# Feature attention enters with two tiles summed, and the last stage's first products in another order and rotation of banks

## The chip, the cores and the metric

The kernel runs on one core of one Trainium2 chip. A core has a matmul engine (TensorE, PE in the profile; its weight loads are PEld), a vector engine (VectorE, DVE), an activation engine (ScalarE, ACT), a general engine (GpSimd, POOL) and a queue engine that here only starts transfers (SyncE, SP). The metric is the device time of one execution in microseconds. All times in the rows below are microseconds from the start of one profiled execution.

## The reference: what is computed

Eight layers are applied to x, a residual of 1024 tokens by 256 features, each as x = x + layer(layernorm(x)). The three that the change touches are the last ones:

```
# layer 5: mixture of 8 experts, top 2, y = W2(silu(W1 x) * (W3 x)) for each
out = sum over the two experts of weight * y
# layer 6: attention over the feature axis
qk = einsum('bdm,bdn->bmn', qh, kh) * scale
ret = einsum('bmn,bcn->bcm', softmax(qk), vh)
# layer 7: product-key memory beside a gated MLP
routing = hidden @ W_q against 2 x 64 keys, top 8 of each side, top 8 of the 64 sums
ew = silu(x @ down_embed[indices]) * softmax(scores)
out = (silu(x @ gate_w) * (x @ up_w)) @ down_w + ew @ up_embed[indices]
```

## The kernel before, in words

The program is straight-line code for five engines, each with an instruction stream of its own in hand-written order; they are tied by counting semaphores. The tokens are eight tiles (t = 0 to 7) of 128. The residual X stays in SBUF. The semaphore `x_tile` counts tiles of X that a stage has finished, eight for each.

**End of the experts (layer 5).** The last expert rows are scattered to DRAM (`yg`), and SP brings them back in token order, one transfer for each tile (`sp_last`, L894), into a ring of four places; the fifth and later wait until a place was consumed. DVE then adds, for each tile, two weighted rows to X: `combine(t)`, two `scalar_tensor_tensor` of 128x256, L1063 and L1064, the second after a wait for the first. `combine` is handed to the next stage if `k.front.get(6)` is true. Layer 6 sets `k.front[6] = {}` when it is built; an empty dictionary counts as false in Python. So in the kernel before, all eight `combine(t)` run at the end of layer 5, and `x_of(t)` in layer 6 does nothing.

**Feature attention (layer 6).** For each tile there are four units u (32 in all), and for each unit four scores steps on PE (`scores`, L2326) whose row maxima DVE takes (`top`, L2181, 128x512 out of a bank). Five units of scores (20 steps, `FRONT`) are made before the first unit's softmax; the steps from the 17th on share three banks, so that a step waits for the `top` three steps earlier. DVE's order is: `x_of(0)`, the layernorm statistics of tile 0 (L262 to L264), `x_of(1)`, the normalisation of tile 0 (L281, after POOL's L270 made 1/sqrt), statistics of tile 1, the 20 `top`, `x_of(2)`, `x_of(3)`, and then per unit u four more `top` in two halves, with `rest(u, half)` behind each half; its first line is `x_of(u + 4)` behind the second half of units 0 to 3. PE turns scores for exponentials (`turned`, L2351), and multiplies by the values (L2372). POOL makes masked copies of keys (L2111) and queries (L2118) and folds in the maxima (`less`, L2126).

**Last stage (layer 7).** A gate-up unit n (16 of them: eight for the first 512 tokens, eight for the others, `gate_up(n)`) is two products of 128x512, gate and up, each two matmuls of 128 rows deep; every float32 matmul stands in the trace as two records, so a unit is 8 records, half a unit 4. They go to two banks: `SETS[n % 3]` is bank 0, 2 or 6. ACT makes `silu(n)` (L2682), DVE `product(n)` (L2554), which frees the banks and counts up `h`. `embed(n)`, 4 records, is the product with the expert table, followed by `silu_e(n)` on ACT (L2686). `project(n)` makes the queries (banks 6 and 7, then `q_ps`), ACT copies them (L2714), PE multiplies them by the keys in 32 small matmuls (L2823, banks 6 and 7 again), ACT copies the result (L2718, `r_sb`). DVE's order is fixed: product 0, then for each half of the tiles `sides`, a product, `both`, a product, `places`, a product (so products 1, 2, 3 and then 4, 5, 6 lie between the steps of the top-8 search), then `hot(0)`, product 7 and so on. ACT takes part in this: table loads for `exp`, and `hot` (L2703, L2707), two at a time between the silus. `front_turn(e, 7)` is the transposition of the last tile (L2492), `front_rows` the copy behind it (L2502). `mm` (L354) is the helper that issues every gate-up, project and embed matmul.

The weights of the last stage (4.2 MB) are loaded by SP as soon as `x_tile` says that layer 5 is complete.

Of the kernel before, what the change touches and what calls it, by code (L numbers as in the profile page):

```python
# [21 lines left out]
ALU = mybir.AluOpType  # L22
ACT = mybir.ActivationFunctionType
AX = mybir.AxisListType

P = 128
# [324 lines left out]
def mm(e, out, pairs, start=True, stop=True):  # L351

    for n, (a, b) in enumerate(pairs):
        ins = e.matmul(out, a, b, start=start and n == 0, stop=stop and n == len(pairs) - 1)  # L354
    return ins
# [419 lines left out]
def experts(k, l, F, chunk, row, base, shared_expert, prefix):  # L775
# [164 lines left out]
    def dve(e):  # L940
# [123 lines left out]
            e.scalar_tensor_tensor(k.X[:, t], both[:, 1], wB[:, t:t + 1], k.X[:, t], ALU.mult, ALU.add)\  # L1064
                .then_inc(k.x_tile, 1)

        if not shared_expert and k.front.get(6):
            k.front[6]["combine"] = combine
            return
        for t in range(NT):  # L1070
# [946 lines left out]
def feature_attention(k, l):  # L2017
# [146 lines left out]
    def dve(e):  # L2164
        ch = k.chain(e, "dve")
        front = k.front.get(7)

        def norm(t):
            if t >= 2:
                after(e, "s_ps", STEPS * UNITS * (t - 1))  # L2170
                after(e, "xm", t - 1)
            ln_norm_dve(e, k, at0 + t, t, t % 2).then_inc(k.ln_out, 1)

        def top(u, r):
            t, b, jp = halves(u)
            step = STEPS * u + r
            if t >= 2 and u % UNITS == 0 and r == 0:
                after(e, "nt_ps", t - 1)
            after(e, "s_ps", step + 1)
            c = r * R + 2 * G * (1 - jp)  # L2180
            e.tensor_reduce(nm[t % 2][:, b, c:c + 2 * G:G],  # L2181
                            k.bank[:, step_bank(step), :].rearrange("p (j n) -> p j n", j=2), AX.X, ALU.max,
                            negate=True).then_inc(S["mx"], 1)

        def inverse(t, half):
            after(e, "od", t + 1)
            c = slice(half * P, (half + 1) * P)
            ch.step(e.reciprocal(rec[:, c], od[:, D + half * P:D + (half + 1) * P]))

        def quotient(t):  # L2190
            e.tensor_tensor(tmp, od[:, 0:D], rec, ALU.mult).then_inc(S["v_sb"], 1)

        def final(t):
            after(e, "v_sb", t + 1)
            e.tensor_tensor(k.X[:, t, :], k.X[:, t, :], tmp, ALU.add).then_inc(k.x_tile, 1)

        def rest(u, half):

            t, n = divmod(u, UNITS)
            if half == 1 and u < UNITS:  # L2200
                x_of(u + 4)
            if n == 0 and half == 0 and t + 2 < NT:
                ln_stats_dve(e, k, ch, t + 2, t % 2)
            if n == 1 and half == 0 and t + 2 < NT:
                norm(t + 2)
            if n == 2 and t > 0:
                inverse(t - 1, half)
            if n == 3 and t > 0:
                quotient(t - 1) if half == 0 else final(t - 1)
            if front:  # L2210
                for f, tiles in front["dve_behind"].get((u - LAST, half), ()):
                    for t in tiles:
                        front[f](e, t)

        def x_of(t):

            if k.front.get(6):
                k.front[6]["combine"](t)
                e.wait_ge(k.x_tile, done0 - NT + t + 1)

        e.wait_ge(k.masks, masks0 + 2)
        x_of(0)
        ln_stats_dve(e, k, ch, 0, 0)
        x_of(1)
        norm(0)
        ln_stats_dve(e, k, ch, 1, 1)
        for u in range(FRONT):
            for r in range(RG):
                top(u, r)
            if u == 0:  # L2230
                norm(1)
        x_of(2)
        x_of(3)
        for u in range(NU):
            ahead = [(n, r) for n in units_ahead(u) for r in range(RG)]
            for half in (0, 1):
                for n, r in ahead[half * len(ahead) // 2:(half + 1) * len(ahead) // 2]:
                    top(n, r)
                rest(u, half)
        inverse(NT - 1, 0)  # L2240
        inverse(NT - 1, 1)
        quotient(NT - 1)
        final(NT - 1)
        if front:
            front["stats"](e, NT - 1)
            front["norm"](e, NT - 1)
# [189 lines left out]
def peer_mlp(k, l):  # L2436
# [67 lines left out]
    if l >= 6:  # L2504
# [2 lines left out]
                                      (3, 0): (("stats", (4, 5)), ("norm", (0, 1))), (3, 1): (("norm", (2, 3)),),  # L2507
                                      (5, 1): (("norm", (4, 5)), ("stats", (6,)), ("norm", (6,)))})

    def rows(j, h):  # L2510

        return g["out"].rearrange("(j p h) d -> j h p d", p=P, h=2)[bass.ds(j, 1), h].rearrange("j p d -> p (j d)")
# [35 lines left out]
    def dve(e):  # L2548
        ch = k.chain(e, "dve")

        def product(n):
            half, ib = n // IB, n % IB
            e.wait_ge(S["silu"], n + 1)
            e.tensor_tensor(hT[:, half, ib], sg[n % 3], k.bank[:, SETS[n % 3] + 1, :], ALU.mult).then_inc(S["h"], 1)  # L2554

        def sides(b):
            for u in range(UB * b, UB * b + UB):
# [119 lines left out]
    def act(e):  # L2677
        def silu(n):
            e.wait_ge(S["g_ps"], n + 1)
            if n >= 3:  # L2680
                e.wait_ge(S["h"], n - 2)
            e.activation(sg[n % 3], k.bank[:, SETS[n % 3], :], ACT.Silu).then_inc(S["silu"], 1)  # L2682

        def silu_e(n):
            e.wait_ge(S["e_ps"], n + 1)
            e.activation(eT[:, n // EB, n % EB], k.bank[:, SETS[n % 3], :], ACT.Silu).then_inc(S["e_sb"], 1)  # L2686

        def exp(b):
            r = slice(UB * b, UB * b + UB)
# [55 lines left out]
        for n in range(24, MINE * NT, 2):  # L2745
            hot(n, 2)

    def gate_up(e, n):
        half, ib = n // IB, n % IB
        if n == IB:  # L2750
            e.wait_ge(S["e_sb"], EB)
        if n == 2:
            e.wait_ge(S["r_sb"], 2)
        if n >= 3:
            e.wait_ge(S["h"], n - 2)
        for b in (0, 1):
            ins = mm(e, k.bank[:, SETS[n % 3] + b, :],
                     [(wgu[:, kb, 2 * (ib // 4) + b, ib % 4 * P:(ib % 4 + 1) * P],
                       k.XNT[:, kb, HALF * half:HALF * half + HALF]) for kb in range(KB)])
        ins.then_inc(S["g_ps"], 1)  # L2760

    def project(e, n):
        e.wait_ge(k.xt_sb, at0 + 4 * (n + 1) + CREDIT)
# [3 lines left out]
    def pe_first(e):  # L2767

        e.wait_ge(S["ld"], 16 * 6)
        e.wait_ge(k.xt_sb, at0 + 4 + CREDIT)  # L2770
        gate_up(e, 0)
        front_turn(e, 6)
        e.wait_ge(k.f6_out, k.f6_out_at)
        project(e, 0)
        gate_up(e, 1)
        front_turn(e, 7)
        project(e, 1)

    def pe(e):
        bank = k.bank  # L2780

        def embed(n):
            half, eb = n // EB, n % EB
            if n in (0, 1):
                e.wait_ge(S["h"], IB - 1 + n)
            elif n in (4, 5, 6):
                e.wait_ge(S["h"], 2 * IB - 6 + n)
            elif n in (3, 7):
                e.wait_ge(S["e_sb"], n - 2)
            mm(e, bank[:, SETS[n % 3], :], [(de[:, kb, eb * P:(eb + 1) * P], k.XNT[:, kb, HALF * half:HALF * half + HALF])  # L2790
                                          for kb in range(KB)]).then_inc(S["e_ps"], 1)

        def turn_w(u):
# [24 lines left out]
        for h in (0, 1):  # L2818
# [3 lines left out]
                    at, q = j * 2 * K + side * K, side * HALF + j * P  # L2822
                    ins = e.matmul(bank[:, QB + h, at:at + K], qT[r, q:q + P], keys[r, side], start=True, stop=True)  # L2823
            ins.then_inc(S["k_ps"], 1)
        for n in range(2, IB):
            gate_up(e, n)
        for n in range(EB):
            embed(n)
# [161 lines left out]
```

## Time and profile before

| | before |
|---|---|
| median of 3 runs (lowest, highest) | 1143.98 us (1141.27, 1144.33) |
| the profiled execution | 1145.51 us, of which the span of the profile is 1143.8 |
| PE busy in the span | 1036.3 us (91%) |
| DVE busy | 572.9 us (50%) |
| mean granted clock of PE | 0.94 of full speed |
| first `combine` of layer 5 | 832.69 |
| first scores matmul of layer 6 | 843.84 |
| first gate-up unit of the last stage | 1000.36 |
| last DVE instruction | 1141.22 |

The profile is one execution, 1.5 us above the median of the others. Busy shares are averages over eight stages with different limits, so each edit has to be read in its own stage: who waits there, and for whom. The granted clock has two levels, 0.5 (1.2 GHz) and 1.0 (2.4 GHz); a stretch that shows something between saw both.

### The profile page before, as it was taken

The page shows a single profiled execution, that of the slowest core. Times are in us where ns is not written, and L with a number is a line of the kernel's source. Part 1 is how long each engine was busy: PE and PEld are TensorE (multiplying, and loading weights), DVE is VectorE, ACT ScalarE, POOL GpSimd, SP SyncE. Part 2 cuts the span into 40 slices and gives each one's busy share as a digit, 9 for nine tenths or more (in the row PEclk, how much of TensorE's full clock was granted, in tenths as well). Part 3 has the DMA queues.
Part 4 walks back from the last instruction along what each step waited for, and adds up shares of the span by engine and source line. Part 5 has one row for each costly group of instructions (what it writes and reads, how often), then busy time and mean ns, then how long its engine had stood idle before and what let it go on. Part 6 is the DMA issues. An engine that isn't in the chain of part 4 may idle for free.

```text
span 1143.8 us, 17531 instructions
## 1 busy us (share of the span) xinstructions
PE 1036.3 (91%) x6658; PEld 693.6 (61%) x6658; DVE 572.9 (50%) x1312; ACT 367.9 (32%) x687; POOL 258.7 (23%) x330
## 2 busy tenths in 40 slices
PE   5879999989999999979774999999849999998989
PEld 4666699457666767658653677777613443443467
DVE  6986423543434343455385112122166778556791
ACT  3652233232212121204210222122104666736660
POOL 4321431600000000003531222222132453202350
PEclk9995999999999999989985999999956999988999
DMA  9002032210101010065026112101060000020000
GB/s 285 27 2 101 19 97 84 88 38 29 38 14 38 24 38 5 11 229 226 1 99 223 28 33 102 37 28 42 19 227 1 2 1 1 2 73 1 0 10 28
DMA packets 37433, 67.26 MB, mean 59 GB/s; under 512 B 4456, under 2 KB 27080, under 8 KB 35816
## 3 DMA queue, kind: packets, MB, share of 16 engines
q1 hardware_dynamic: 29960, 51.98, 13.4%
q0 software_dynamic: 4080, 11.15, 3.4%
q10 hardware_dynamic: 3312, 3.02, 0.8%
q8 instruction: 56, 0.92, 0.3%
q14 instruction: 25, 0.20, 0.1%
HBM read 54.72 MB, written 11.40 MB: 58 GB/s over the span
## 4 chain that ended last, share of the span: by engine, by line
PE 76%; DVE 14%; ACT 3%; DMA 3%; issue 2%; POOL 2%; SPq 0%; DVEq 0%; ACTq 0%; POOLq 0%
PE bank L354 21%; PE bank L1255 12%; PE bank L1279 7%; PE bank L1605 6%; PE bank L2326 4%; PE bank L2351 3%; PE bank L2372 3%; PE bank L1615 3%; PE bank L2808 2%; PE bank L1268 2%; PE bank L1590 2%; PE bank L1580 2%; PE bank L2390 1%; PE bank L2814 1%; PE bank L1240 1%
## 5 line engine op out<-in xcount | busy, mean ns | idle before, releaser
L1255 PE MATMUL bank<-big 128*128 x552 | 147.7, 417 | 0.6 <-ACT big L1140 0.6
L354 PE MATMUL bank<-XNT,big 128*128 128x512 f32 x296 | 140.7, 626 | 5.4 <-DVE big L2554 2.8
L1255 PEld LDWEIGHTS bank<-big 128*128 128x128 f32 x552 | 98.1, 191 | 39.6 <-issue 2.7
L2326 PE MATMUL bank<-big,xs 32*128 32x512 f32 x256 | 88.5, 739 | 18.7 <-DVE xs L281 17.7
L270 POOL TENSOR_TENSOR rstd<-ve,half 128x1 f32<-128x1 f32 x48 | 27.5, 576 | 331.6 <-DVE ve L264 331.3
L354 PEld LDWEIGHTS bank<-XNT,big 128*128 128x128 f32 x296 | 56.6, 199 | 70.7 <-issue 62.0
L2181 DVE TENSOR_REDUCE big<-bank 128x2 f32<-128x512 f32 x128 | 81.9, 685 | 24.7 <-PE bank L2326 24.1
L1279 PE MATMUL bank<-big 128*128 (+1 forms) x368 | 87.2, 380 | 1.1 <-ACT big L1155 1.1
L1033 DVE TENSOR_TENSOR big<-big,bank 128x704 f32<-128x704 f32 x23 | 20.5, 889 | 124.9 <-ACT big L1148 124.9
L2272 ACT ACTIVATE big<-bank 128x1024 f32<-128x1024 f32 x64 | 64.9, 1024 | 38.9 <-PE bank L2351 38.6
L354 PE MATMUL bank<-CTXT,big 128*128 128x512 f32 (+1 forms) x192 | 67.0, 493 | 10.7 <-DMA big<-wvT 10.7
L1279 PEld LDWEIGHTS bank<-big 128*128 128x128 f32 (+1 forms) x368 | 68.0, 190 | 13.6 <-issue 1.7
L2351 PE MATMUL bank<-big 32*128 32x512 f32 x256 | 69.3, 667 | 1.6 <-POOL big L2126 1.4
L1148 ACT ACTIVATE big<-bank 128x176 f32<-128x176 f32 (+1 forms) x46 | 24.7, 538 | 136.6 <-PE bank L1255 135.8
L1605 PE MATMUL bank<-big 128*128 128x256 f32 x256 | 65.4, 401 | 1.2 <-issue 1.2
L1512 ACT COPY big<-bank 128x1024 f32<-128x1024 f32 x16 | 16.2, 1012 | 145.5 <-PE bank L1615 145.5
L1464 DVE COPY big<-bank 128x512 f32<-128x512 f32 x16 | 11.1, 691 | 99.5 <-PE bank L1590 99.5
L354 PE MATMUL bank<-big,CTXT 128*128 128x256 f32 (+1 forms) x224 | 58.0, 409 | 0.0
L354 PEld LDWEIGHTS bank<-CTXT,big 128*128 128x128 f32 x192 | 32.9, 196 | 40.8 <-issue 40.8
L915 POOL DMA_INDIRECT yg<-big x23 | 22.7, 986 | 150.8 <-DVE big L1046 144.0
L2326 PEld LDWEIGHTS bank<-big,xs 32*128 32x128 f32 x256 | 31.6, 210 | 40.7 <-issue 26.8
L1605 PEld LDWEIGHTS bank<-big 128*128 128x128 f32 x256 | 47.4, 195 | 14.0 <-DVE X L1458 5.4
(351 smaller groups left out, 1807.2 us busy)
## 6 DMA issues: line engine op xcount, KB each, us to landing
big<-m_gu SPq DMA_DIRECT2D x8, 1408.0 KB
big<-m_d SPq DMA_DIRECT2D x8, 768.0 KB
big<-a_qk SPq DMA_DIRECT2D x16, 256.0 KB, 2.9
yg<-big ACTq DMA_DIRECT2D x23, 128.0 KB
big<-m_gu SPq DMA_DIRECT2D x8, 352.0 KB
big<-a_o SPq DMA_DIRECT2D x16, 128.0 KB, 2.1
xn<-XNT SPq DMA_DIRECT2D x8, 256.0 KB, 5.9
big<-f_keys SPq DMA_DIRECT2D x1, 2048.0 KB, 9.1
```

The costliest lines, as they stand in the source:

```text
L270: e.tensor_tensor(k.rstd[at % NT][:, :], k.ve[at % NT][:, :], k.half[:, 0:1], ALU.pow).then_inc(k.ln_rstd, 1)
L354: ins = e.matmul(out, a, b, start=start and n == 0, stop=stop and n == len(pairs) - 1)
L1148: tell(e.activation(dst, src, ACT.Silu), "hs")
L1255: ins = e.matmul(out, xgT[s % 2][:, kb, :], WB[:, bass.ds(at[s] + (kb * 2 * F + c * chunk), chunk)], start=kb == 0, stop=kb == KB - 1)
L1279: ins = e.matmul(bank[:, Y[s % 2], 0:D], hT[s % 2][0:row, b, :], WB[0:row, bass.ds(at[s] + (WGU + b * D), D)], start=b == 0, stop=b == NB - 1)
L1605: ins = e.matmul(bank[:, QK0 + j % 2, q * D:(q + 1) * D], cT[:, t * P:(t + 1) * P], wo[h % 2], start=True, stop=True)
L1615: ins = e.matmul(bank[:, CB + b, t * SEQ:(t + 1) * SEQ], v[rows(b), h % FIRST, t], pT[rows(b), t], start=True, stop=True)
L2181: e.tensor_reduce(nm[t % 2][:, b, c:c + 2 * G:G], k.bank[:, step_bank(step), :].rearrange("p (j n) -> p j n", j=2), AX.X, ALU.max, negate= ...
L2272: e.activation(pt[u % 2][:, r].rearrange("p r j n -> p r (j n)"), k.bank[:, b:b + 2, :], ACT.Exp, scale=float(G) ** -0.5).then_inc(S["ex"], 1)
L2326: e.matmul(bank[:, step_bank(step), :], k.xs[t % 2][q, b * P:(b + 1) * P], cm[t % 2][q, 2 * jp:2 * jp + 2].rearrange("p j n -> p (j n)"), ...
L2351: ins = e.matmul(bank[:, pair_banks(u, pair) + r % 2, :], cr[q, t, jp, nb * P:(nb + 1) * P], xm[t % 2][q, 2 * jp:2 * jp + 2].rearrange("p ...
L2372: ins = e.matmul(bank[r * R:(r + 1) * R, VB, jp * D:(jp + 1) * D], cv[t % 2][:, nb, r * J + 2 * jp + j], pt[u % 2][:, r, j], start=nb == 0 ...
```

## The change

Two parts. First, the test `k.front.get(6)` becomes `6 in k.front` in both places: layer 5 hands over `combine` and returns, and layer 6 makes the sums itself, tiles 0 and 1 at its start, 2 and 3 behind the 20 `top`, and 4 to 7 one behind each of the units 0 to 3. Second, in the last stage, the banks of the gate-up units and of the embed products rotate in another order, half of unit 1 and the transposition of tile 7 change places, and the first half of unit 2 is issued ahead of the product with the keys. The waits follow: unit 2 needs product 0 (it uses banks 0 and 1 now) and no longer the copied routing scores, which unit 3 now waits for; the first embed product needs product 5 and not 6.

```diff
-        if not shared_expert and k.front.get(6):
+        if not shared_expert and 6 in k.front:
             k.front[6]["combine"] = combine
             return
@@
         def x_of(t):
-            if k.front.get(6):
+            if 6 in k.front:
                 k.front[6]["combine"](t)
                 e.wait_ge(k.x_tile, done0 - NT + t + 1)
@@
+    def unit_banks(n):
+        return SETS[n if n < 2 else (0, 2, 1)[(n - 2) % 3]]
+    def embed_bank(n):
+        return SETS[(0, 2, 1)[n % 3 if n < EB else (n + 1) % 3]]
@@ product, silu, silu_e: SETS[n % 3] becomes unit_banks(n), embed_bank(n)
-    def gate_up(e, n):
+    def gate_up(e, n, part=(0, 1)):
-        if n == IB:
-            e.wait_ge(S["e_sb"], EB)
-        if n == 2:
-            e.wait_ge(S["r_sb"], 2)
-        if n >= 3:
-            e.wait_ge(S["h"], n - 2)
-        for b in (0, 1):
+        if 0 in part:
+            if n == IB:
+                e.wait_ge(S["e_sb"], EB)
+            if n == 2:
+                e.wait_ge(S["h"], 1)
+            if n == 3:
+                e.wait_ge(S["r_sb"], 2)
+            if n >= 4:
+                e.wait_ge(S["h"], n - 2)
+        for b in part:
...
-        ins.then_inc(S["g_ps"], 1)
+        if 1 in part:
+            ins.then_inc(S["g_ps"], 1)
@@ pe_first
         project(e, 0)
-        gate_up(e, 1)
+        gate_up(e, 1, (0,))
         front_turn(e, 7)
+        gate_up(e, 1, (1,))
         project(e, 1)
+        gate_up(e, 2, (0,))
@@ embed
-            if n in (0, 1):
-                e.wait_ge(S["h"], IB - 1 + n)
+            if n in (0, 1, 2):
+                e.wait_ge(S["h"], IB - 2 + n)
@@ behind the products with the keys
-        for n in range(2, IB):
+        gate_up(e, 2, (1,))
+        for n in range(3, IB):
             gate_up(e, n)
```

## Rows read from the trace of the kernel before

**Rows 1.** The page, chain of work that ended last, shares of the span.

```profile
PE 76%; DVE 14%; ACT 3%; DMA 3%; issue 2%; POOL 2%; SPq 0%; DVEq 0%; ACTq 0%; POOLq 0%
```

**Rows 2.** Timeline, entry of layer 6: start, us, engine, line, [idle before, releaser].

```profile
832.69 0.48 DVE L1063 SCALAR_TENSOR_TENSOR X<-XNT,big,X 128x256 f32<-128x256 f32 x1 [6.12 <-DMA XNT<-yg]
833.21 0.48 DVE L1064 SCALAR_TENSOR_TENSOR X<-XNT,big,X 128x256 f32<-128x256 f32 x1
...
841.71 0.42 DVE L262 BATCH_NORM_STATS2 st<-X 128x6 f32<-128x256 f32 x1
...
842.49 0.15 DVE L264 TENSOR_SCALAR ve<-mv 128x1 f32<-128x1 f32 x1
...
843.33 0.41 DVE L281 TENSOR_SCALAR xs<-X,mv,rstd 128x256 f32<-128x256 f32 x1 [0.68 <-POOL rstd L270]
...
843.84 5.74 PE L2326 MATMUL bank<-big,xs 32*128 32x512 f32 x22 [17.73 <-DVE xs L281]
```

**Rows 3.** Busy time by stretch in layer 6; behind POOL the granted clock, DMA share, GB/s.

```profile
843.80:856.30 12.50, 10.20 (x32) 4.84 (x32) 10.95 (x20) 0.00 (x0) 9.15 (x20) 0.64 0.84 332
856.30:863.60 7.30, 6.52 (x23) 2.68 (x24) 2.58 (x4) 3.36 (x6) 4.33 (x3) 0.50 0.00 0
863.60:872.50 8.90, 8.90 (x26) 3.82 (x25) 6.67 (x13) 1.94 (x2) 0.56 (x1) 0.50 0.00 0
872.50:890.00 17.50, 17.50 (x147) 5.80 (x146) 11.67 (x21) 11.43 (x15) 6.49 (x8) 0.92 0.00 1
```

**Rows 4.** Timeline of layer 6 where the late sums would stand, DVE and POOL.

```profile
860.94 1.89 POOL L2111 TENSOR_TENSOR big<-big,strip 128x1024 f32<-128x1024 f32 x1
...
863.70 1.89 DVE L2181 TENSOR_REDUCE big<-bank 128x2 f32<-128x512 f32 x3 [1.12 <-PE bank L2326]
...
875.63 1.29 DVE L2181 TENSOR_REDUCE big<-bank 128x2 f32<-128x512 f32 x2 [2.36 <-PE bank L2326]
...
884.70 1.29 DVE L2181 TENSOR_REDUCE big<-bank 128x2 f32<-128x512 f32 x2 [0.49 <-PE bank L2326]
884.77 1.28 POOL L2126 TENSOR_TENSOR big<-big 128x512 f32<-128x512 f32 x1 [1.72 <-ACT big L2262]
```

**Rows 5.** Timeline of the last stage's first 25 us.

```profile
1009.85 1.98 PE L354 MATMUL bank<-XNT,big 128*128 128x512 f32 x4 [0.46 <-ACT XNT L2502]
...
1011.87 0.61 ACT L2714 COPY big<-bank 128x512 f32<-128x512 f32 x1 [1.56 <-PE bank L354]
...
1012.62 3.82 PE L2823 MATMUL bank<-big 64*128 64x64 f32 x32 [0.79 <-ACT big L2714]
...
1017.09 0.23 DVE L2558 MAX8 big<-big 128x8 f32<-128x64 f32 x1 [9.96 <-ACT big L2718]
...
1024.05 0.69 DVE L2554 TENSOR_TENSOR big<-big,bank 128x512 f32<-128x512 f32 x1 [1.41 <-ACT big L2682]
```

**Rows 6.** The chain that ended last, 1000 to 1061 us: start, us, what.

```profile
1000.36 3.43 PE bank L354 x8
...
1017.11 6.21 PE bank L354 x8
...
1035.50 0.69 DVE big L2554
...
1042.61 0.61 DVE big L2554
1043.27 6.79 PE bank L354 x8
...
1050.67 1.22 ACT big L2703 x2
...
1054.16 7.13 PE bank L354 x16
```

**Rows 7.** One line's instructions (ns least/median/most), and POOL's timeline beside it.

```profile
L2594 DVE TENSOR_TENSOR big<-big x2: 191/1061/1931, 1029.2 to 1040.7; 128x32 f32<-128x32 f32 x2
...
1040.22 2.34 POOL L2544 TENSOR_TENSOR big<-big 128x1024 f32<-128x1024 f32 x1 [34.03 <-ACT big L2707]
```

More of the change, by code:

```diff
@@ L2553, in product @@
             e.wait_ge(S["silu"], n + 1)
-            e.tensor_tensor(hT[:, half, ib], sg[n % 3], k.bank[:, SETS[n % 3] + 1, :], ALU.mult).then_inc(S["h"], 1)
+            e.tensor_tensor(hT[:, half, ib], sg[n % 3], k.bank[:, unit_banks(n) + 1, :], ALU.mult).then_inc(S["h"], 1)
         def sides(b):
@@ L2681, in silu @@
                 e.wait_ge(S["h"], n - 2)
-            e.activation(sg[n % 3], k.bank[:, SETS[n % 3], :], ACT.Silu).then_inc(S["silu"], 1)
+            e.activation(sg[n % 3], k.bank[:, unit_banks(n), :], ACT.Silu).then_inc(S["silu"], 1)
         def silu_e(n):
             e.wait_ge(S["e_ps"], n + 1)
-            e.activation(eT[:, n // EB, n % EB], k.bank[:, SETS[n % 3], :], ACT.Silu).then_inc(S["e_sb"], 1)
+            e.activation(eT[:, n // EB, n % EB], k.bank[:, embed_bank(n), :], ACT.Silu).then_inc(S["e_sb"], 1)
         def exp(b):
@@ L2746, in act @@
             hot(n, 2)
-    def gate_up(e, n):
+    def gate_up(e, n, part=(0, 1)):
         half, ib = n // IB, n % IB
-        if n == IB:
-            e.wait_ge(S["e_sb"], EB)
-        if n == 2:
-            e.wait_ge(S["r_sb"], 2)
-        if n >= 3:
-            e.wait_ge(S["h"], n - 2)
-        for b in (0, 1):
-            ins = mm(e, k.bank[:, SETS[n % 3] + b, :],
+        if 0 in part:
[8 more added lines that the diff above has]
+        for b in part:
+            ins = mm(e, k.bank[:, unit_banks(n) + b, :],
                      [(wgu[:, kb, 2 * (ib // 4) + b, ib % 4 * P:(ib % 4 + 1) * P],
                        k.XNT[:, kb, HALF * half:HALF * half + HALF]) for kb in range(KB)])
-        ins.then_inc(S["g_ps"], 1)
+        if 1 in part:
+            ins.then_inc(S["g_ps"], 1)
     def project(e, n):
@@ L2789, in embed @@
                 e.wait_ge(S["e_sb"], n - 2)
-            mm(e, bank[:, SETS[n % 3], :], [(de[:, kb, eb * P:(eb + 1) * P], k.XNT[:, kb, HALF * half:HALF * half + HALF])
+            mm(e, bank[:, embed_bank(n), :], [(de[:, kb, eb * P:(eb + 1) * P], k.XNT[:, kb, HALF * half:HALF * half + HALF])
                                           for kb in range(KB)]).then_inc(S["e_ps"], 1)
```

## The prediction, made before the change was run

> **What bounds the kernel now.** I read the chain that ended last first: three quarters of it is PE [rows 1]. But the change touches only two places where PE is not the bound, so the answer lies in the timeline there. At the entry of layer 6, PE stands still for 17.73 us: DVE waits for the first returned expert row, sums tile 0 from 832.69, and comes to the statistics of tile 0 only at 841.71, behind all eight sums, though they need tile 0 alone; the first scores matmul is at 843.84 [rows 2]. In the last stage the chain changes engine at 1024.05, where DVE waits 1.41 us for the silu of unit 2; from there it is DVE's, through product 5 at 1035.50 to product 6 at 1042.61; PE, out of work, takes up the embed products at 1043.27 and, by way of ACT, unit 8 at 1054.16 [rows 5, 6]. The third view is the granted clock: half speed from 856.3 to past 872.5, because PE was nearly idle before and then waits for banks; only then nearly full [rows 3].
>
> **The dead test.** The dictionary is empty when it is first tested, so before the change nothing is handed over. With the new test the sums of tiles 1 to 7 move. I take them in DVE's order.
>
> Entry. A sum is two dependent instructions, 833.21 - 832.69 = 0.52 us apart, so 1.04 us a tile [rows 2]. Tile 0 is done at 832.69 + 1.04 = 833.73, and the statistics follow at once, 7.98 us earlier than at 841.71. Between the last statistics instruction (842.49 + 0.15 = 842.64) and the normalisation (843.33) DVE idles 0.69 us for POOL's reciprocal root [rows 2]; the sum of tile 1 goes in there with 1.04 us, 0.35 more than the gap. I add 0.5 for POOL's small instruction and the sum getting in each other's way. First scores matmul at 843.84 - 7.98 + 0.85 = 836.7: **7.1 us gained**. It can't be more than 7.98. The weights of the last stage are loaded when the eighth sum is done, now some 35 us later, about 165 us before their first use (1000.36 [rows 6]); that delay costs nothing. With the cover gone it would cost the load's length, about 12 us (DMA share 0.84 in the 12.5 us from 843.8 [rows 3]).
>
> What the six other sums take back (6 x 1.04 = 6.2 us of DVE):
> - Tiles 2 and 3 stand behind the 20th maximum, in front of the one at 863.70. DVE idles 1.12 us before it, so it ended at 862.58; POOL's L2111 runs until 862.83. The two sums end at 862.83 + 2.08 = 864.9, 1.2 late [rows 4]. From here to 872.5 PE's scores at half clock go round three banks, each step waiting for a maximum, and DVE is busy 6.67 of 8.9 us [rows 3]; a delay at the head of such a ring is passed on in full. Cost 1.2.
> - Tile 4 falls ahead of 875.63, where DVE idled 2.36 us [rows 4] and only 0.4 us of normalisation shares the gap. Cost 0.
> - Tiles 5 to 7 fall between pairs of maxima, 872.5 to 890. DVE is busy 11.67 of 17.5 us there [rows 3], idle 0.49 before the pair at 884.70 [rows 4], the sum 1.04. Each overruns by about 0.5, and PE, which is never idle there, can absorb a part. Tile 7 would run beside POOL's L2126 of 884.77 [rows 4], and such neighbours block each other: L2594 takes 0.19 us once and 1.93 the other time, ending as POOL's 1040.22 + 2.34 does [rows 7]. Its second half waits up to 1.3 us. Cost 0.4 + 0.4 + 0.9 = 1.7.
>
> So 2.9 is taken back, **4.2 us net**. Bounds: nothing beyond the 1.2 (net 5.9), and all 6.2 us plus the 1.3 us block (7.5, net -0.4, nothing gained).
>
> The Trainium skill, SBUF — State Buffer, section "SBUF: two separate sides", says the same of the block as a lock: a VectorE instruction with two SBUF inputs and a GpSimd instruction hold a shared port pair for their whole length, and the later one stands still. By that rule every sum that meets POOL pays; with the rule left aside and the sums sliding through beside POOL, the give-back would be 0.25 + 0.9 less and the net 5.3 instead of 4.2. The row on L2594 agrees with the lock.
>
> **The last stage.** At full clock 8 records take 3.43 us, 4 take 1.72 [rows 6].
> - The transposition of tile 7 moves ahead of half a unit, so ACT's copy lies beside PE's work. PE's wait of 0.46 us before project(1) goes: it starts at 1009.4 [rows 5].
> - The first half of unit 2 follows it. Its wait is for product 0, long made. project(1) ends streaming 1.72 us later, 1011.1; the half unit ends at 1012.8; ACT's copy (1011.87 before, 1011.4 now, 0.61 long) is done by then. The 32 small matmuls start at 1012.85 instead of 1012.62 and end at 1016.7 instead of 1016.44 [rows 5]. So the top-8 search starts **0.2 us later** (1017.3).
> - The second half of unit 2 runs at 1016.7 without a wait and ends at 1018.4, at 1020.1 if the clock is down. Before, the whole unit and the next came after 1017.11, took 6.21 us for 8 records that are worth 3.43 [rows 6], and the silu of unit 2 was there just before 1024.05. Now it is there at about 1019.3 (1021 with a slow clock), before DVE wants product 2 at 1022.6 + 0.2. DVE's wait of 1.41 goes, less 0.2: **1.2 us gained** on DVE's chain either way [rows 5].
> - Products 3, 4, 5 then come 1.2 earlier with DVE as the bound, product 5 at 1034.3. Units 6 and 7 wait for products 3 and 4 as before; PE is through unit 7 near 1035.7, and embed(0), which now needs product 5 alone, follows at once and ends near 1037.5. Before, it was the first half of the 6.79 us that began at 1043.27 [rows 6]: at half clock **3.4 us** taken out of the stretch behind product 6.
> - Product 6. DVE's own chain puts it at 1042.61 - 1.2 = 1041.4. POOL's 2.34 us instruction moves too (ACT's `hot` comes some 2 us earlier), and it may block DVE's small steps in another place: 1041 to 1042. I take 1041.4.
> - PE is then idle for about 4 us, so the clock falls, as it had after the shorter wait before. Embed 1 to 3 are 12 records: 7 at half clock (6.0) and 5 at full (2.1) end at 1042.1 + 8.1 = 1050.2, silu 0.7: unit 8 at about 1051. Against 1054.16 this is 3.2. ACT's four `hot` instructions (from 1050.67 [rows 6]) no longer stand between the second and third silu_e at the end, but under embed(2), which itself waits for product 7. I take **3.0 us**. Bounds: 1.2 + 0.5 (only DVE's part and the wait) = 1.7 below, and 5.5 if the clock stays up and the 12 records take 5.2.
>
> Behind unit 8 the banks and waits come out as before, so the rest shifts as a block.
>
> **Sum.** 4.2 + 3.0 = 7.2 us. On the profiled span: 1143.8 - 7.2 = 1136.6 (its own time 1145.51, so 1138.3). The median of the runs is 1.5 below that execution; 1143.98 - 7.2 = **1136.8 us**. Because those runs lie 3.1 us apart, I call 0.3% (3.4 us) the least that can be told from no change.
>
> **Rivals.**
> 1. *The sums take everything back.* DVE is the bound from 843.8 on and the six sums cost their length and the block. For it: 10.95 of 12.5 us busy [rows 3]. Against: none of the six stands in that stretch. Time 1143.98 + 0.4 - 3.0 = 1141.4. Chance 0.08.
> 2. *The last stage gains nothing*, as POOL's instruction moved onto DVE's steps holds product 6 at 1042.6 and the colder PE pays for embed(0). For it: the 1.93 of L2594 [rows 7]. Against: embed(0) is out of the way. 1143.98 - 4.2 = 1139.8. Chance 0.13.
> 3. *More than forecast:* the clock rises earlier in layer 6. From 863.6 to 872.5 PE takes 8.9 us at half clock where DVE has 6.67 us of work [rows 3]; at full clock DVE would set the pace, 2.2 less. With 4.5 in the last stage: 1143.98 - 4.2 - 2.2 - 4.5 = 1133.1. Chance 0.15.
> 4. *Slower:* the clock stays down in layer 6. It rose only shortly after 872.5, where the full mix of matmuls began [rows 3]; if the pauses of PE for the sums of tiles 5 to 7 keep it down, each microsecond of work costs one more, since PE is busy all of the 17.5 us there [rows 3]. 7.2 us of such work undo the gain; from 10.6 us of it on (21 us of further half clock) the kernel is over 3.4 us slower. For the whole stretch, at its clock of 0.92: 1136.8 + 0.84 x 17.5 = 1151.5. Against: PE has no idle there, and the sums add only tenths. Chance 0.03.
>
> The forecast itself has 0.61, with its own range 1134.5 to 1139.5. Rivals 1 and 4 are left outside the range, and half of 3's tail: **1132.0 to 1140.6**. Faster by over 0.3%: below 1140.5, the forecast, rival 3 and most of rival 2: 0.87. Within 0.3%: rival 1 and the rest: 0.10. Slower: 0.03.
>
> **What would show it.** First L1063 near 832.7, then L262 near 833.7, first L2326 near 836.7; eight sums spread to about 878; the 21st maximum 1 us behind its old distance from the entry; the first sort of layer 6 (PE L2390) 4 us earlier. In the last stage, unless shifted: no DVE wait at product 2, four L354 records ahead of L2823, embed(0) ahead of product 6, unit 8 about 3 us closer to unit 0 (53.8 us before). Wrong it would be through a longer half-clock stretch after 863, a stall of PE at the sums of tiles 5 to 7 of over 1 us each, or L2594 blocked again.

## The result, and the profile after

The changed kernel takes 1135.42 us (median of 5 runs, 1134.34 to 1137.76) against 1143.98 of before, timed beside it (5 runs, 1141.27 to 1148.46); the ratio is 0.9931, 95% interval 0.9911 to 0.9951. Measured once more it was 0.9947 (0.9929 to 0.9965). The forecast was 1136.8 us, 7.2 less; by the two ratios the measured gain is 7.9 and 6.1 us. The profiled execution took 1134.34, its span 1132.6. Ratios compare undisturbed executions: one of the six of experiment 8's kernel took 4096 us, for a cause that nothing on record shows, and is left out.

The page of the changed kernel: its first line, and the chain that ended last by engine. It answers to [rows 1]: PE's share of the chain fell, DVE's rose.

```profile
span 1132.6 us, 17536 instructions
...
PE 73%; DVE 17%; issue 3%; DMA 3%; ACT 2%; POOL 2%; SPq 0%; DVEq 0%; ACTq 0%; POOLq 0%
```

**Entry of layer 6**, the timeline of DVE and then of PE, in answer to [rows 2]. In all the rows below, `...` stands for lines left out.

```profile
831.14 0.48 DVE L1063 SCALAR_TENSOR_TENSOR X<-XNT,big,X 128x256 f32<-128x256 f32 x1 [6.44 <-DMA XNT<-yg]
831.66 0.48 DVE L1064 SCALAR_TENSOR_TENSOR X<-XNT,big,X 128x256 f32<-128x256 f32 x1
832.18 0.43 DVE L262 BATCH_NORM_STATS2 st<-X 128x6 f32<-128x256 f32 x1
...
833.56 0.48 DVE L1064 SCALAR_TENSOR_TENSOR X<-XNT,big,X 128x256 f32<-128x256 f32 x1
834.08 0.41 DVE L281 TENSOR_SCALAR xs<-X,mv,rstd 128x256 f32<-128x256 f32 x1
```

```profile
834.59 2.09 PE L2326 MATMUL bank<-big,xs 32*128 32x512 f32 x8 [10.35 <-DVE xs L281]
```

The statistics stand 1.04 us behind the first sum, where they stood 9.02 behind it. The second sum fills DVE's wait for POOL's reciprocal root, and the normalisation follows it without a gap. From the first sum to the first scores matmul it is 3.45 us instead of 11.15 [rows 2].

**The late sums**, DVE's timeline and one line of POOL's, in answer to [rows 4].

```profile
853.25 0.62 DVE L1063 SCALAR_TENSOR_TENSOR X<-XNT,big,X 128x256 f32<-128x256 f32 x1
...
854.94 0.48 DVE L1064 SCALAR_TENSOR_TENSOR X<-XNT,big,X 128x256 f32<-128x256 f32 x1
855.46 1.89 DVE L2181 TENSOR_REDUCE big<-bank 128x2 f32<-128x512 f32 x3
...
867.19 1.29 DVE L2181 TENSOR_REDUCE big<-bank 128x2 f32<-128x512 f32 x2 [1.32 <-PE bank L2326]
...
872.50 0.49 DVE L1064 SCALAR_TENSOR_TENSOR X<-XNT,big,X 128x256 f32<-128x256 f32 x1
873.38 1.29 DVE L2181 TENSOR_REDUCE big<-bank 128x2 f32<-128x512 f32 x2 [0.40 <-PE bank L2326]
...
876.73 0.48 DVE L1064 SCALAR_TENSOR_TENSOR X<-XNT,big,X 128x256 f32<-128x256 f32 x1
876.87 1.48 POOL L2126 TENSOR_TENSOR big<-big 128x512 f32<-128x512 f32 x1 [1.68 <-ACT big L2262]
```

Counted from the first scores matmul, the 21st maximum comes at 20.87 (855.46 - 834.59) where it came at 863.70 - 843.84 = 19.86: 1.0 is given back at the head of the ring. The pair of 867.19 is 0.8 late; the wait ahead of it shrank from 2.36 to 1.32, which is the sum of tile 4. The sum of tile 7 (its second half at 876.73) meets POOL's L2126, but it is the earlier of the two: it takes its usual 0.48 us, and POOL 1.48 where it took 1.28.

**The last stage**, from the chain that ended last, and POOL's timeline beside it, in answer to [rows 6, 7]. The first L354 line is unit 0, the next the embed products 1 to 3, the last unit 8; L2561 is `product` here (the two shown are products 2 and 6), L2595 and L2598 are two of DVE's small steps.

```profile
993.26 3.43 PE bank L354 x8
...
1015.28 0.69 DVE big L2561
...
1030.95 2.07 DVE big L2595
...
1033.05 0.19 DVE big L2596
...
1033.26 1.13 DVE big L2598
...
1034.92 0.61 DVE big L2561
...
1035.57 8.03 PE bank L354 x12
...
1044.27 7.13 PE bank L354 x16
```

```profile
1030.61 2.35 POOL L2551 TENSOR_TENSOR big<-big 128x1024 f32<-128x1024 f32 x1 [31.52 <-ACT big L2714]
1033.04 1.31 POOL L2553 TENSOR_TENSOR big<-big 128x512 f32<-128x512 f32 x1
```

Product 2 stands in the chain of DVE without a wait. Unit 8 comes 1044.27 - 993.26 = 51.0 us behind unit 0, 53.8 before. But two small DVE steps, usually of 0.2 us, end within 0.06 us of POOL's instructions (1033.02 against 1030.61 + 2.35 = 1032.96, 1034.39 against 1033.04 + 1.31 = 1034.35), so product 6 is only 0.6 us nearer to unit 0 (41.66 against 42.25). The embed products, 12 records, take 8.03 us behind a pause of 5.42.

### The profile page after: what moved, and what is told of

The parts are those of the page before. It is cut to its first block, busy times and chain, and to the rows that moved or that the text cites. A ratio compares the mean times of both kernels' runs of the same rounds, so it can differ in the third digit from the quotient of the medians.

```text
span 1132.6 us, 17536 instructions
## 1 busy us (share of the span) xinstructions
PE 1028.8 (91%) x6658; PEld 687.2 (61%) x6658; DVE 574.8 (51%) x1312; ACT 368.4 (33%) x687; POOL 258.8 (23%) x330
## 3 DMA queue, kind: packets, MB, share of 16 engines
q0 software_dynamic: 4080, 11.15, 3.5%
## 4 chain that ended last, share of the span: by engine, by line
PE 73%; DVE 17%; issue 3%; DMA 3%; ACT 2%; POOL 2%; SPq 0%; DVEq 0%; ACTq 0%; POOLq 0%
PE bank L354 20%; PE bank L1255 13%; PE bank L1279 7%; PE bank L1605 6%; PE bank L2326 5%; PE bank L2351 3%; PE bank L2372 3%; PE bank L1615 3%; PE bank L1268 2%; PE bank L1590 2%; PE bank L2821 2%; PE bank L1580 2%; PE bank L2390 1%; DVE big L2608 1%; DMA big<-yg,big 1%
## 5 line engine op out<-in xcount | busy, mean ns | idle before, releaser
L354 PE MATMUL bank<-XNT,big 128*128 128x512 f32 x296 | 136.3, 609 | 6.9 <-DVE big L2561 5.4
L354 PEld LDWEIGHTS bank<-XNT,big 128*128 128x128 f32 x296 | 55.0, 193 | 69.8 <-issue 59.1
L354 PE MATMUL bank<-CTXT,big 128*128 128x512 f32 (+1 forms) x192 | 67.0, 493 | 11.0 <-DMA big<-wvT 11.0
L354 PE MATMUL bank<-big,CTXT 128*128 128x256 f32 (+1 forms) x224 | 57.9, 409 | 0.0
L354 PEld LDWEIGHTS bank<-CTXT,big 128*128 128x128 f32 x192 | 32.9, 196 | 41.2 <-issue 41.1
```

## The experiments

Every kernel was profiled once and timed in five rounds. The table gives, for each profiled execution, four distances read from the timelines: from the first sum to the first scores matmul, from there to unit 0 of the last stage, from unit 0 to unit 8, and from unit 8 to the end of the span. (The timeline puts unit 0 0.16 us earlier than the chain does, so 51.17 here is the 51.0 above, and 53.96 the 53.8.) The ratio is to the kernel before, timed beside it.

| execution | entry | to unit 0 | to unit 8 | to the end | ratio (95%) |
|---|---|---|---|---|---|
| before | 11.15 | 156.36 | 53.96 | 89.64 | |
| before again | 10.20 | 156.79 | 52.60 | 88.29 | 1.0003 (0.9984 to 1.0022) |
| second part alone | 10.34 | 156.72 | 50.41 | 90.92 | 0.9998 (0.9981 to 1.0015) |
| second part alone, again | 10.77 | 156.34 | 50.31 | 89.53 | 0.9993 (0.9975 to 1.0011) |
| rotation alone | 10.32 | 156.70 | 50.17 | 90.92 | 0.9985 (0.9968 to 1.0001) |
| first part alone | 3.45 | 158.70 | 52.65 | 89.65 | 0.9932 (0.9910 to 0.9954) |
| first part alone, again | 3.45 | 158.63 | 50.87 | 88.23 | 0.9946 (0.9930 to 0.9963) |
| changed | 3.45 | 158.51 | 51.17 | 88.33 | 0.9931 (0.9911 to 0.9951) |
| changed again | 3.45 | 158.57 | 51.29 | 88.32 | 0.9947 (0.9929 to 0.9965) |
| sums in gaps | 3.44 | 157.11 | 50.35 | 89.53 | 0.9926 (0.9903 to 0.9949) |
| sums early | 3.45 | 162.92 | 50.65 | 89.44 | 0.9987 (0.9973 to 1.0000) |
| POOL later | 3.45 | 158.57 | 47.59 | 88.28 | 0.9924 (0.9907 to 0.9941) |
| PE kept busy | 3.45 | 158.14 | 49.29 | 89.49 | 0.9944 (0.9927 to 0.9961) |
| all together | 3.45 | 157.09 | 46.47 | 88.33 | 0.9888 (0.9860 to 0.9916) |

**1. The first part alone.** The kernel before with

```diff
-        if not shared_expert and k.front.get(6):
+        if not shared_expert and 6 in k.front:
@@
-            if k.front.get(6):
+            if 6 in k.front:
```

> The kernel before with the first part of the change alone (both tests of the dictionary). Theory (the two parts add up, each by its own mechanism): the changed kernel's trace gives 11.15 - 3.45 = 7.7 us from the first sum to the first scores matmul, and takes 2.15 back before the last stage, so 5.5 us net: 1138.4 us, ratio about 0.995; first L1063 to first scores matmul 3.45 us, unit 0 of the last stage 158.7 us behind the first scores matmul, and 53.8 us from unit 0 to unit 8 as before. Rival (the late sums take everything back and the gain is all the last stage's): 1144, ratio 1.000. Rival (the gain is all the sums'): 1135.5, ratio 0.993.

Entry and way to unit 0 are the changed kernel's to 0.2 us. The gain is 7.8 us where 5.5 were expected, as much as the whole change has: 0.9932. The interval holds 0.995 and 0.993, so neither the theory nor the second rival is out. From unit 0 to unit 8 it is 52.65 and not 53.96: DVE's wait at product 2, 1.41 us in [rows 5], is 0.61 here with the same code. It was run again beside the changed kernel.

> The first part alone once more. Theory: 5.2 us faster than before, ratio 0.9955. Rival (the first part is the whole gain, as the first comparison had it, 0.9932): 0.993.

0.9946, between the two, and the interval holds both. The whole change, run beside it, had 0.9947: in the times the second part adds nothing to the first.

**2. The second part alone.** The changed kernel with both tests set back to `k.front.get(6)`.

> The kernel before with the second part alone (the last stage's order and banks). Theory: from unit 0 to unit 8 51.0 us instead of 53.8, and up to 1.3 behind unit 8, so 2.8 to 4.1 us: 1140.5 us, ratio about 0.997; no wait of DVE at product 2. Rival (no gain, the search on DVE sets product 6 and what the embed products save is lost to the clock): 1144, ratio 1.000.

> The second part alone once more. Theory: 2.5 us faster than before, ratio 0.998; the granted clock falls at the last embed product or not, which decides over up to 3 us of the end (unit 0 to the end 141.3 with the dip, 139.5 without). Rival (nothing, as the first comparison had it, 0.9998): 1.000.

In both traces unit 8 comes at 50.4 and 50.3 behind unit 0, a little earlier than the theory's 51.0, and DVE doesn't wait at product 2. In the times it is not to be seen: 0.9998 and 0.9993, so between 2.2 us faster and 1.7 slower, and between 2.9 faster and 1.3 slower. The first comparison leaves out the theory's 0.997 and had the rival; the second holds both 0.998 and 1.000. Some of the difference is behind unit 8, where the forecast had seen only a block that shifts. PE's timeline of the second part alone, then of the changed kernel, at the last transposition before the down products (L2811), the last embed product (L354) and the first down product (L2821):

```profile
1087.54 0.66 PE L2811 MATMUL bank<-ident,big 128*128 128x128 f32 x4 [2.65 <-DVE big L2616]
1088.03 3.04 PE L354 MATMUL bank<-XNT,big 128*128 128x512 f32 x4
1091.75 5.53 PE L2821 MATMUL bank<-big 128*128 128x256 f32 x16 [0.69 <-ACT big L2693]
```

```profile
1083.55 0.66 PE L2811 MATMUL bank<-ident,big 128*128 128x128 f32 x4 [2.66 <-DVE big L2616]
1084.04 1.88 PE L354 MATMUL bank<-XNT,big 128*128 128x512 f32 x4
1086.61 3.72 PE L2821 MATMUL bank<-big 128*128 128x256 f32 x16 [0.69 <-ACT big L2693]
```

The wait ahead is the same, 2.65 and 2.66 us. In one execution the clock falls and the two pieces (the embed product and the down product) take 3.04 + 5.53 = 8.57 us, in the other it stays and they take 5.60.

**3. The rotation alone.** The second part alone, with the early half of unit 2 and the split of unit 1 taken back:

```diff
-        gate_up(e, 1, (0,))
-        front_turn(e, 7)
-        gate_up(e, 1, (1,))
-        project(e, 1)
-        gate_up(e, 2, (0,))
+        gate_up(e, 1)
+        front_turn(e, 7)
+        project(e, 1)
@@
-        gate_up(e, 2, (1,))
-        for n in range(3, IB):
+        for n in range(2, IB):
```

> The second part with the new rotation of the banks and its waits, but unit 1 whole and unit 2 whole behind the products with the keys, as before. Theory: the early half unit keeps the clock up and makes product 2 ready, the rotation gives embed(0) ahead of product 6; here the clock falls again beside the 32 small matmuls (granted 0.5 in some of the 8 us behind them), DVE waits about 0.8 us at product 2, and embed(0) still comes early: 1.5 to 2.5 us faster than before, so 1141.8, ratio 0.998. Rival (the gain is the early half unit's): 1144, ratio 1.000, embed(0) early or not.

0.9985, 1.7 us faster, within what was expected, though the interval reaches 1.0001; unit 8 is at 50.17, no later than with the early half. The expected wait of DVE at product 2 did not come, though the clock fell as expected (0.67 in the four microseconds from 1012, product 2 is at 1017.6). Unit 2 starts here as soon as the 32 small matmuls are through (1011.32), without the wait of 0.68 us for the copied scores that stands ahead of it in all four executions of the old order: with the new banks unit 3 has that wait. So what the second part gains, if anything, comes with the banks and their waits; moving the half unit adds nothing that shows.

**4. The kernel before, again.**

> The kernel before once more, unchanged: a second profiled execution of it, and what the comparison says of no change. Open is why the second part of the change shows 2.5 us in the traces and next to nothing in the times. Theory (the profiled execution of before had an unlucky clock in the last stage, 143.6 us from unit 0 to the end, where the first part alone had 142.3 and 139.1 without any edit there): this one lies between 139 and 142.5, and the ratio is 1.000 within 0.002. Rival (143.6 is what this stage takes in before, and the second part's gain is real but lost in the times elsewhere): 143.6 within 0.3.

The theory held: the ratio is 1.0003, and the last stage takes 140.9 us here (52.60 + 88.29), 143.6 in the execution on which the forecast was made, 142.3 and 139.1 in the two of the first part alone, which has the same code there. PE's timeline of this execution and then of the first part alone, again, behind the pause that ends with product 6 (embed products, then unit 8):

```profile
1043.05 8.78 PE L354 MATMUL bank<-XNT,big 128*128 128x512 f32 x16 [2.79 <-DVE big L2554]
1052.51 7.13 PE L354 MATMUL bank<-XNT,big 128*128 128x512 f32 x16 [0.69 <-ACT big L2686]
```

```profile
1037.71 1.98 PE L354 MATMUL bank<-XNT,big 128*128 128x512 f32 x4 [2.79 <-DVE big L2554]
1040.66 5.42 PE L354 MATMUL bank<-XNT,big 128*128 128x512 f32 x12 [0.97 <-DVE big L2554]
1046.77 7.13 PE L354 MATMUL bank<-XNT,big 128*128 128x512 f32 x16 [0.69 <-ACT big L2686]
```

The pause is 2.79 us in both and in the first profile of before. Here the four embed products take 8.78 us, there 1.98 + 5.42 with a wait between; in the first profile of before 10.21. So a part of what the second part seemed to win from 53.96 was the clock of that one execution.

A second thing shows when the four executions of the old order are laid beside the new one. In the first part alone, DVE's timeline at product 2, at the long L2594 and at product 6, and then POOL's:

```profile
1016.79 0.69 DVE L2554 TENSOR_TENSOR big<-big,bank 128x512 f32<-128x512 f32 x1 [0.61 <-ACT big L2682]
...
1033.41 1.94 DVE L2594 TENSOR_TENSOR big<-big 128x32 f32<-128x32 f32 x1
1035.27 0.68 DVE L2554 TENSOR_TENSOR big<-big,bank 128x512 f32<-128x512 f32 x1
```

```profile
1032.96 2.35 POOL L2544 TENSOR_TENSOR big<-big 128x1024 f32<-128x1024 f32 x1 [32.77 <-ACT big L2707]
1035.38 1.27 POOL L2546 TENSOR_TENSOR big<-big 128x512 f32<-128x512 f32 x1
```

Product 6 stands 41.07 us behind unit 0 here (1035.27 - 994.20) and 41.08 when run again, 42.34 and 42.41 in the two executions of before. In the changed kernel it is 41.74 and 41.91, in the second part alone 41.88 and 41.90. From product 2 to product 6 it is 18.5 us in all four executions of the old order and 19.6 to 19.7 in these four: the old order has one of POOL's additions ahead of product 6, and the second begins when product 6 has begun (1035.38); the new order has both ahead of it.

**5. Where a late sum costs.** Two kernels, each the changed one with late sums moved. `sums in gaps`: tiles 2 and 3 behind the 16th maximum, 5 behind the normalisation of tile 2; 4, 6 and 7 stay where the change has them, so three of the six move. `sums early`: 2 to 4 behind the 8th maximum, 5 to 7 behind the 12th. The edit of `sums in gaps`, then that of `sums early`:

```diff
-            if half == 1 and u < UNITS:
-                x_of(u + 4)
+            if (u, half) in ((0, 1), (2, 1), (3, 1)):
+                x_of(4 + u)
@@
+            if u == 1 and half == 0:
+                x_of(5)
@@
             if u == 0:
                 norm(1)
-        x_of(2)
-        x_of(3)
+            if u == UNITS - 1:
+                x_of(2)
+                x_of(3)
```

```diff
-            if half == 1 and u < UNITS:
-                x_of(u + 4)
@@
-        x_of(2)
-        x_of(3)
+            if u in (1, 2):
+                for t in (2, 3, 4) if u == 1 else (5, 6, 7):
+                    x_of(t)
```

> The changed kernel with the six late sums moved to where DVE is idle: tiles 2 and 3 behind the 16th maximum (DVE idles 2.78 us there), 4 where it is, 5 behind the normalisation of tile 2 (1.32 idle), 6 and 7 behind units 2 and 3. Theory (the 2.15 us given back are waits of PE for maxima behind the sums, above all the two at the head of the three-bank ring): first scores matmul to unit 0 of the last stage 157.0 instead of 158.7, 1.6 us faster than the changed kernel: 1133.8, ratio to before 0.9915. Rival (the give-back is the clock's, not the sums' place): no change, 1135.4.

> The changed kernel with all six late sums in the stretch where DVE takes maxima back to back (tiles 2 to 4 behind the 8th maximum, 5 to 7 behind the 12th). Theory (there DVE sets the pace and a sum costs its length; where they stand now most of it is hidden): first scores matmul to unit 0 of the last stage 158.5 - 2.15 + 6.2 = 162.6, 4 us slower than the changed kernel: 1139.5, ratio to before 0.9965. Rival (a sum costs the same anywhere, or PE's half clock hides it): 158.5 and 1135.4.

To unit 0 it is 157.11 and 162.92 where 157.0 and 162.6 were expected. DVE's timeline of `sums in gaps` at the 17th maximum: the two sums end before PE has the next scores, and DVE still waits.

```profile
847.56 0.47 DVE L1063 SCALAR_TENSOR_TENSOR X<-XNT,big,X 128x256 f32<-128x256 f32 x1
...
849.10 0.49 DVE L1064 SCALAR_TENSOR_TENSOR X<-XNT,big,X 128x256 f32<-128x256 f32 x1
850.49 1.89 DVE L2181 TENSOR_REDUCE big<-bank 128x2 f32<-128x512 f32 x3 [0.90 <-PE bank L2329]
```

The six sums cost 6.3 us in the stretch where DVE sets the pace (162.92 less 156.6, the mean of the five without them), 2.0 where the change has them, 0.5 with three of them moved into gaps. In the times `sums early` has given back nearly all of the gain, 0.9987 (0.9973 to 1.0000), more than the 0.9965 expected; `sums in gaps`, 0.9926, can't be told from the changed kernel, to which the trace has it 1.4 us faster.

**6. POOL and DVE.** The changed kernel, with a wait that only delays:

```diff
             e.wait_ge(S["oh"], MINE * u + 4)
+            if u == 0:
+                e.wait_ge(S["h"], IB)
```

> The changed kernel with one wait more: POOL makes its first pair of sums of the last stage only when product 7 is done. Theory (POOL's 2.35 and 1.31 us instructions stop DVE's small steps ahead of product 6: 2.06 and 1.13 us where 0.19 and 0.18 are usual): product 6 comes 2.8 earlier, 38.9 behind unit 0 instead of 41.7, unit 8 between 46.5 and 48.3 instead of 51.2 by the clock; 1131 to 1133, ratio 0.990. Rival (those steps are long of themselves, or the time returns behind unit 8 where DVE is the bound): product 6 at 41.7, or unit 8 early and the same time from unit 0 to the end, 139.5.

Timeline of DVE at product 6 (L2563 here) and the two small steps ahead of it that stood for 2.07 and 1.13 us (L2597 and L2600 here); then POOL's:

```profile
1033.48 0.19 DVE L2597 SCALAR_TENSOR_TENSOR big<-big 128x32 f32<-128x32 f32 x1
...
1033.92 0.18 DVE L2600 TENSOR_SCALAR big<-big 128x32 f32<-128x32 f32 x1
...
1034.55 0.68 DVE L2563 TENSOR_TENSOR big<-big,bank 128x512 f32<-128x512 f32 x1
...
1038.83 2.73 DVE L2616 TENSOR_TENSOR big<-big 128x512 f32<-128x512 f32 x1
```

```profile
1037.80 3.21 POOL L2553 TENSOR_TENSOR big<-big 128x1024 f32<-128x1024 f32 x1 [36.18 <-DVE big L2563]
```

Product 6 starts 38.92 behind unit 0, 38.9 expected, 41.74 before this wait. The blocking has not gone: it holds DVE at 1038.83 now (2.73 us for 0.69), behind the products that PE waits for. Unit 8 comes 3.6 us earlier and nothing is lost behind it (88.28 us to the end). The clock fell here too, behind a pause of 2.61 us: the 12 records of embed products took 7.25. The ratio of 0.9924 (0.990 was expected) is lower than both of the changed kernel's, by 0.8 and 2.6 us, less than the trace's 3.6, and the intervals overlap: the trace shows the gain, the times alone do not.

The Trainium skill, SBUF — State Buffer, section "SBUF: two separate sides", says that a VectorE instruction with two SBUF inputs, or in one of its two-port modes, and a GpSimd instruction contend for one shared pair of ports under an exclusive lock: whichever starts first holds it to its end, and the other stands still. The rows agree: the ends coincide to 0.06 us at both places in the changed kernel. Whether the one-input L2598 runs in such a mode no row shows.

**7. The clock in the pause.** The changed kernel with five matmuls between embed(0) and embed(1) whose result nobody reads; it computes the same.

```diff
             embed(n)
+            if n == 0:
+                for _ in range(5):
+                    e.matmul(bank[:, 5, :], de[:, 0, 0:P], k.XNT[:, 0, 0:HALF], start=True, stop=True)
```

> The changed kernel with five matmuls more on PE (128x512, into a free bank, read by nobody) between embed(0) and embed(1), where PE idles 5.4 us. It computes the same. Theory (the clock falls in that pause and the 12 records behind it take 8.0 us instead of 5.2): the granted clock stays at 1.0 and the embeds end when product 7 lets them: unit 8 at 49.1 behind unit 0 instead of 51.2, 2 us faster than the changed kernel: 1133.4. Rival (the clock there costs nothing, because embed(2) waits for product 7 anyway): unit 8 at 51.2, 1135.4; or the added work is in the way: later.

PE's timeline (the added ones are L2845), and the granted clock by stretch (the figure behind POOL's) in this kernel and then in the changed one:

```profile
1032.81 4.45 PE L2845 MATMUL bank<-XNT,big 128*128 128x512 f32 x10
1038.40 1.98 PE L354 MATMUL bank<-XNT,big 128*128 128x512 f32 x4 [1.14 <-DVE big L2561]
1040.82 3.70 PE L354 MATMUL bank<-XNT,big 128*128 128x512 f32 x8 [0.44 <-DVE big L2561]
1045.21 7.13 PE L354 MATMUL bank<-XNT,big 128*128 128x512 f32 x16 [0.69 <-ACT big L2693]
```

```profile
1038.00:1042.00 4.00, 3.16 (x7) 1.35 (x8) 3.97 (x8) 1.58 (x3) 0.00 (x0) 1.00 0.00 0
```

```profile
1035.00:1044.00 9.00, 8.02 (x12) 3.14 (x12) 5.46 (x9) 3.90 (x7) 1.49 (x1) 0.68 0.01 2
```

Unit 8 at 49.29, 1.9 us earlier, as the theory had it. The time shows no gain (0.9944, between the changed kernel's 0.9931 and 0.9947, where 2 us were expected). In the profiled execution the clock fell at the second pause instead, and the end took 89.49 for 88.33; whether that is so in the others isn't known.

**8. All together.** Experiments 5 (gaps), 6 and 7 (three matmuls, the pause being shorter), and three more such matmuls ahead of the last transposition. Beside it, the changed kernel again.

> The changed kernel with the late sums in DVE's gaps, POOL's first sums of the last stage behind product 7, three idle matmuls in the pause behind embed(0), and three in the pause of 2.65 us ahead of the transposition before the last embed product. Theory (each takes its own piece: 1.5, 3.6, 1.3 and 0 to 3 by the clock): first scores matmul to unit 0 157.1; unit 8 46.3 behind unit 0; clock 1.0 through the last embed product and down(0); unit 0 to the end 134.5; about 1129, ratio 0.988. Rival (the pieces overlap, or the added matmuls get in the way): 1132 or more, no better than the wait of POOL alone.

> The changed kernel once more, beside each part alone on the same chip. Theory (in the traces the first part gives 4.9 to 5.5 us, the second 2.5): ratio to before 0.993 again, and faster than the first part alone by 2.5 us. Rival (the second part gives nothing in time): equal to the first part alone.

All together: 0.9888 (0.9860 to 0.9916) where 0.988 was expected, 12.8 us faster than before and 6.7 less than the changed kernel run beside it (0.9947), and the two intervals don't overlap. The traces: 157.09, 46.47 and 88.33. The changed kernel again had the rival's outcome: 0.9947 is not 2.5 us faster than the first part alone, 0.9946. PE's timeline at the second pause, with the added matmuls as L2859, the last embed product (1.88) and down(0) (3.72) at full clock. The changed kernel has the same 1.88 and 3.72 without added matmuls, so these rows don't show that they were needed there:

```profile
1079.22 2.74 PE L2859 MATMUL bank<-XNT,big 128*128 128x512 f32 x6
1082.03 0.66 PE L2816 MATMUL bank<-ident,big 128*128 128x128 f32 x4
1082.52 1.88 PE L354 MATMUL bank<-XNT,big 128*128 128x512 f32 x4
1085.09 3.72 PE L2826 MATMUL bank<-big 128*128 128x256 f32 x16 [0.69 <-ACT big L2698]
```

## Why the prediction was right, and where not

**The time.** 1136.8 was forecast, 1135.4 measured, with the right sign and size. That the sum came so near is in part luck, two errors of opposite sign: the first part gives more than its 4.2, the second less than its 3.0.

**Entry, 7.1 us.** Right in its mechanism; that it is right to the tenth is luck. The five executions without the new test give 11.15, 10.20, 10.34, 10.77 and 10.32, mean 10.56, and the nine with it 3.45: 10.56 - 3.45 = 7.1. The term had two errors within it that cancel: the 0.5 for POOL and the second sum did not occur (3.45, not 4.0), and the execution forecast from had an entry 0.6 longer than the mean. The five differ by DVE's waits for returned rows between the eight sums, 1.37 us in that execution and 0.43 to 1.04 in the others. The weights of the last stage went out 35 us later, as said (877.24 against 841.82), and cost nothing; but by the prediction's own numbers that is some 124 us before their use and not 165, and it measured 116.

**Taken back, 2.9 us.** Over-sized: 158.6 - 156.6 = 2.0. The 1.2 at the head of the ring measured 1.0. The 1.7 for tiles 5 to 7 was too much by 0.7: the 0.9 for tile 7 held a block of its second half by POOL, and here the sum was the earlier of the two, so POOL waited (0.2 us) and DVE did not. That the place decides is shown by experiment 5 from both sides, 0.5 and 6.3. The net of the first part is 5.1 in the traces; the two timings say 7.8 and 6.2, with intervals down to 5.3 and 4.2.

**The last stage, 3.0 us.** Over-sized. From unit 0 to the end, the four executions with the old order take 143.6, 140.9, 142.3 and 139.1, mean 141.5; the four with the whole second part (alone and changed, twice each) 141.3, 139.8, 139.5 and 139.6, mean 140.1. That is 1.4, with a scatter as large, and the two ratios of the second part alone, 0.9998 and 0.9993, say 0.5 (some 2 faster to 1 slower, taken together). Its size is not settled further. The means can be split into the terms of the sum.

*DVE's chain, 1.2 us.* This is the step that failed: "DVE's wait of 1.41 goes, less 0.2: 1.2 us gained on DVE's chain either way", with product 6 taken at 1041.4. The wait at product 2 went, but it was 1.41 in that execution only, 1.94 in the second one of before and 0.61 in both of the first part alone, with the granted clock in the four microseconds from 16 us behind unit 0 at 0.50 in the first two, and at 0.65 and 0.64 in the others. And behind product 5 the time was lost again: POOL's first addition comes earlier (37.5 to 37.7 us behind unit 0, 38.8 to 40.1 in the old order), and two additions now hold DVE's steps ahead of product 6 where one did before (18.5 us from product 2 to product 6 became 19.6 to 19.7). The prediction had seen that POOL might block in another place and left it inside a range of 1041 to 1042. Product 6 stands at 41.7 behind unit 0 in the mean of the old order's four and 41.9 in the mean of the four with the second part: nothing gained, and against the first part alone 0.7 to 0.8 lost. Experiment 6 shows the blocking to be the cause: 2.8 us, both blocks. That fits the times, in which the second part adds nothing to the first.

*The embed products, about 2.0 us of the 3.2.* Right in the mean: from product 6 to unit 8 the old order takes 11.6, 10.2, 11.6 and 9.8, mean 10.8, the new one 9.4, 9.4, 8.5 and 8.4, mean 8.9; the forecast had 9.6 for the changed kernel. But "the clock falls, as it had after the shorter wait before" took the clock's fall for a constant of before. It is not: behind the same 2.79 us the embed products took 10.21, 8.78, 10.16 and 7.40 us of PE's work in the four executions of the old order. With the whole second part, and POOL not delayed, the pause at product 6 is 4.2 to 5.6 us, and the clock fell in all six such executions. So the second part takes embed(0) out and has a fallen clock for the rest each time. The upper bound of 5.5 is too low by the prediction's own figures: 1042.1 + 5.2 + 0.7 = 1048.0, 6.2 ahead of 1054.16.

*Behind unit 8, nothing.* "The rest shifts as a block" leaves out a second pause, of 2.65 us, behind which the clock falls in some executions and not in others: 88.2 to 90.9 us to the end, in the old order as in the new (means 89.0 and 89.3).

**Rivals.** The first is out: the sums don't take all back. The third and the fourth are out too, since the clock rose at its usual place in layer 6, some 32 us behind the first scores matmul in both kernels (0.50 before it; 0.92 in the 17.5 us of [rows 3], 0.90 in the same stretch after). The second (the last stage gains nothing, 1139.8) had the right stage and, with POOL's instruction on DVE's steps, the right cause; its total is wrong, since the first part gave more.

## What to carry to other kernels

Test for a key with `in`, not for the truth of the value: here an empty dictionary had switched off an overlap worth some 5 us in the traces. When work is moved into another stage, put it where the trace shows its engine waiting: the same six sums cost 0.5, 2.0 or 6.3 us by place alone. When a chain of small steps gets earlier, look for what the other engine's instructions will now fall on: here two of POOL's additions took back what the removed wait had given, and one semaphore wait moved them away. Price a matmul pause by more than one execution: one profile may hold a lucky or an unlucky clock, and two profiles of the same code were 2.7 us apart in one stage.

## What was not expected of the hardware

The granted clock of PE behind a pause of some 2.7 us is not reproducible: 2.79 us ahead of the embed products and 2.65 ahead of the last transposition were followed by half speed in some executions and full speed in others of identical code (before 3.56 us for the last embed product, before again 1.88). Ahead of the embed products it fell in each of the six executions with a pause of 4.23 to 5.60 us (the 12 records behind it took 6.99 to 8.03 us), and also in the two with 2.42 (rotation alone, 7.11) and 2.61 (POOL later, 7.25). With matmuls that nobody reads in the pause it was 1.00 through the whole stretch of experiment 7, in the one execution profiled.

Of POOL's two-input additions and DVE's instructions of 128x32 elements the later stands until the earlier ends: 2.07 us for 0.19, and also a one-input instruction (L2598), 1.13 for 0.18. It goes both ways: in experiment 6 POOL's addition at 1037.80, begun while DVE ran one of 128x1024 elements, took 3.21 us for 2.35.
